# Cross-attention and mixture-of-experts layer: the key-value summary by single heads on four column tiles of TensorE, the read-out by pairs of heads on two row tiles

## The chip, the cores and the metric

The kernel runs on one core of a Trainium2 chip. The metric is device time in microseconds (us), the median of several runs; it is compared with the same kernel before the change.

## What is computed

A layer with two parts, in fp32 throughout. `x` is (4, 512, 512), `ctx` is (4, 1024, 512), there are 16 heads of 32 columns each and 8 experts.

```python
def feature(x): return where(x > 0, x + 1.0, exp(x))
# part 1: linear attention over the context
q, gate = layernorm(x) @ Wq.T, sigmoid(layernorm(x) @ Wg.T + bg)
k, v = split(ctx @ Wkv.T)                      # 16 heads x 32 columns
q, k = feature(q), feature(k)
kv_summary = einsum('bhsd,bhse->bhde', k, v)   # 32 x 32 for each head
k_sum = k.sum(axis=-2)                         # 32 for each head
z = 1.0 / (einsum('bhld,bhd->bhl', q, k_sum)[..., None] + EPS)
attn = einsum('bhld,bhde->bhle', q, kv_summary) * z
x = x + (attn * gate) @ Wo.T
# part 2: two of eight experts for each token
w, sel = top_k(layernorm(x) @ Wr, 2); w = softmax(w)
x = x + sum over the two of w * (layernorm(x) @ We[sel] + be[sel])
```

## The kernel before

The program is written engine by engine, with counting semaphores between the engines. TensorE's order of work is written out by hand in two lists, `KEYS` and `QUERIES`, which every engine walks in the same order. There are four batches. `keys(0)` comes first; then a loop of three rounds does `queries(b)` and `keys(b + 1)`; then `queries(3)`, and after it the expert part, 46 tiles of 128 rows.

`KEYS` goes over the eight context tiles of 128 rows of one batch. For each tile i it has "T c" (four transposes of the next context tile), "P k" and "P v" (the two projections), and "KV" of the tile before. In between stand the transposes "T z", the router's logits "L" (L1105) and the prefix counts "K" (L1111, L1112) of the batch before. A projection is done by `three`: each operand is split into a high and a low fp32r half, and for each of four row blocks there are three matmuls of 512 columns (L1097, L1098, L1099), 12 in all.

"KV" (L1151) adds one context tile to the key-value summary, and does so in plain fp32: four matmuls, one for each group g of four heads. The stationary operand is `khat[:, g*128:(g+1)*128]` (128 rows of context by 128 columns of keys), the moving operand is `vones[:, g, :]`, 132 columns: the four heads' 128 columns of values and four columns of ones, which give the sums of the keys. The result in PSUM (`kvp`, two groups in each of the two banks `kvb`) holds each head's keys against all four heads' values, of which only the four blocks on the diagonal are wanted. After the eighth tile VectorE multiplies it with a 0/1 `mask` into `kvbd` (L882, two operations of 264 columns). GpSimd builds `mask` at the start of the program (L468 to L475).

`QUERIES` has the four query projections "Q", then for four token tiles the gate projection "G", the read-out "A", the transposes "T a" of the attention's output, and the output projection "O". "A" (L1179) does four fp32 matmuls, one for each g: stationary `qhat[:, g, tile]` (128 features by 128 tokens), moving `kvbd[:, g, :]` (132 columns); groups 0 and 1 go to one PSUM bank, 2 and 3 to a second. VectorE then works in `attend` (L885): `den` from the last four columns of each group (L890, two operations), the reciprocal (L894), four operations that scale 128 columns each (L899), and the product with the gate (L904).

An fp32 matmul of the program is two matmul instructions and two weight loads in the profile: the 128 matmuls of "KV" are 256 instructions, the 64 of "A" are 128.

GpSimd, beside the attention, splits the expert weights and stores them to DRAM (`cut_to_dram`, L522), and computes the scales of both layer norms (L498); its first `load_expert` waits for the last of the attention's weights to be split (`w_low`, L539). SyncE (SP) issues the loads. For the expert part it issues, in one queue, the halves of the experts' weights (L373), the zero rows for padding (L365), the row tiles of each expert tile (L360) and the biases (L393).

Of the kernel before, what the change touches and what calls it, by code (L numbers as in the profile page):

```python
# [10 lines left out]
ALU = mybir.AluOpType  # L11
# [3 lines left out]
P = 128  # L15
HEADS = 16
ATTN_EPS = 1e-6
# [3 lines left out]
def xattn_moe_kernel(nc, x, ctx_in, wq_t, wg_t, bg, wkv_t, wo_t, wr, we, be, out):  # L21
# [16 lines left out]
    HG = HEADS // G  # L38
    HD = D // HEADS
    CW = P + HG  # L40
    assert L == D == 512 and ST == 8 and TT == KT == 4 and E == 8


# [13 lines left out]
    with ExitStack() as stack:  # L57
        def sb(name, shape, dt=F32):
            return stack.enter_context(nc.sbuf_tensor(name, shape, dt))
# [32 lines left out]
        BUF = 4 * D + G * 2 * CW + 2 * D  # L92
        buf = sb("buf", [P, BUF])
        ctx_raw = buf[:, 0:4 * D].rearrange("p (s t d) -> p s t d", s=2, t=2)
        vones = buf[:, 4 * D:4 * D + 2 * G * CW].rearrange("p (s g c) -> p s g c", s=2, g=G)
        expk = buf[:, 4 * D + 2 * G * CW:BUF].rearrange("p (s d) -> p s d", s=2)
        expq = expk
        be_all = buf[:, 0:E * D].rearrange("p (e d) -> p e d", e=E)
        khat = sb("khat", [P, 2, D])
        xs_raw = khat  # L100
        kvbd = sb("kvbd", [P, G, CW])
        zeros = sb("zeros", [P, D])
        bias = sb("bias", [P, D])
        y_sb = [kvbd[:, :, :].rearrange("p g c -> p (g c)")[:, 0:D], zeros[:, :]]
# [62 lines left out]
        pj = [stack.enter_context(nc.psum_tensor(f"pj{i}", [P, D], F32)) for i in range(4)]  # L167
        kvb = [stack.enter_context(nc.psum_tensor(f"kvb{i}", [P, D], F32)) for i in range(2)]
        late_z = [a[:, :].rearrange("p (k c) -> p k c", k=KT) for a in kvb]
        kvp = [a[:, 0:2 * CW].rearrange("p (g c) -> p g c", g=2) for a in kvb]  # L170


        w_loaded = [sem(f"w_loaded{i}") for i in range(2 * 4 + 3)]
# [100 lines left out]
        def pj_bank(name, i, second=0):  # L274
            return pj[place(PJ_USES, name, i, second) % 4]
# [158 lines left out]
        def _(pool):  # L434
# [20 lines left out]
            link(nc.gpsimd.affine_select(out=ident[:, :], in_=ident[:, :], compare_op=ALU.not_equal, fill=1.0,  # L455
                                         base=0, pattern=[[-1, P]], channel_multiplier=1))
            link(nc.gpsimd.memset(full[1], 1.0))
            nc.gpsimd.memset(vones[:, :, :, P:CW], 1.0).then_inc(consts, 1)
            nc.gpsimd.memset(mhalf[:, :], -0.5).then_inc(consts, 1)
            nc.gpsimd.memset(nt[:, 0:1], 0.0).then_inc(consts, 1)  # L460
            nc.gpsimd.memset(run[:, :, :], 0.0).then_inc(consts, 1)
# [9 lines left out]
            for ap, pat in ((m4, [[-HD, HG], [0, HD]]), (mask[:, P:CW], [[-HD, HG]])):  # L471
                link(nc.gpsimd.affine_select(out=ap, in_=ap, compare_op=ALU.is_ge, fill=0.0, base=0,
                                             pattern=pat, channel_multiplier=1))
                link(nc.gpsimd.affine_select(out=ap, in_=ap, compare_op=ALU.is_ge, fill=0.0, base=HD - 1,
                                             pattern=[[-s, c] for s, c in pat], channel_multiplier=-1))  # L475
            link(nc.gpsimd.memset(full[0], 0.0))

            link(nc.gpsimd.affine_select(out=full[0], in_=full[0], compare_op=ALU.is_ge, fill=1.0,
# [138 lines left out]
        def _(act):  # L617
# [43 lines left out]
            def keys(b, before_):  # L661
                for step, kind, i in KEYS:
                    if before_ is None and (step, i) in CHUNKS and kind in ("", "z"):
                        high_w(CHUNKS[step, i])
                    elif step == "T":
                        high(kind, b if kind != "z" else before_, i)
                    elif step == "P" and kind == "k":
                        act.wait_ge(SEMS["k"], nth("k", b, i))
                        act.wait_ge(SEMS["kv"], nth("kv", b, i - 2))
                        nc.scalar.activation(khat[:, i % 2, :], pj_bank("expk", i)[:, :], ACT.Relu)  # L670

                        act.wait_ge(SEMS["khat"], nth("khat", b, i - 2)) if i >= 2 else act.wait_ge(SEMS["qhat"], nth("qhat", b, i - 2))
                        nc.scalar.activation(expk[:, i % 2, :], pj_bank("expk", i)[:, :], ACT.Exp).then_inc(SEMS["expk"], 1)  # L673
                    elif step == "P":
                        act.wait_ge(SEMS["v"], nth("v", b, i))
                        act.wait_ge(SEMS["kv"], nth("kv", b, i - 2))
                        nc.scalar.copy(vones[:, i % 2, :, 0:P], pj_bank("v_copied", i)[:, :].rearrange("p (g c) -> p g c", g=G)).then_inc(SEMS["v_copied"], 1)
                        if i == 0 and before_ is not None:
                            norm_x2(before_, TT - 1)
                        if i in (4, 5):  # L680
                            norm_x(b, i - 4, before_)
                        if i == 6:
                            norm_x(b, 2, before_)
                            norm_x(b, 3, before_)
                    elif step == "L":
                        exp_gap(before_, i)
# [87 lines left out]
        def _(dve):  # L774
# [85 lines left out]
            def keys(b, before_):  # L860
                for step, kind, i in KEYS:
                    if before_ is None and (step, i) in CHUNKS and kind in ("", "z"):
                        low_w(CHUNKS[step, i])
                    elif step == "T" and kind != "z":
                        low(kind, b, i)
                    elif step == "P" and kind == "k":
                        dve.wait_ge(SEMS["expk"], nth("expk", b, i))

                        nc.vector.scalar_tensor_tensor(khat[:, i % 2, :], expk[:, i % 2, :], 1.0, khat[:, i % 2, :],  # L869
                                                       ALU.min, ALU.add).then_inc(SEMS["khat"], 1)  # L870
                    elif step == "P":
                        if i in (2, 3):
                            stats_x(b, 2 * i - 4)
                            stats_x(b, 2 * i - 3)
                    elif step == "L":
                        pick_two(before_, i, pj_bank("logit_copied", i))
                    elif step == "K":
                        rank_two(0, before_, i, pj_bank("ranked", i))
                dve.wait_ge(SEMS["kv"], nth("kv", b, ST - 1))
                for h in range(2):  # L880
                    m = mask[:, :].rearrange("p (a c) -> p a c", a=1).broadcast_to((P, 2, CW))
                    last = nc.vector.tensor_tensor(kvbd[:, 2 * h:2 * h + 2, :], kvp[h], m, ALU.mult)  # L882
                last.then_inc(SEMS["kvbd"], 1)

            def attend(b, t):  # L885

                banks = [pj_bank("ag", t, h) for h in range(2)]
                dve.wait_ge(SEMS["at"], nth("at", b, t))
                for h in range(2):
                    last = nc.vector.tensor_scalar(  # L890
                        den[:, t % 2, 8 * h:8 * h + 8].rearrange("p (g c) -> p g c", g=2),
                        banks[h][:, 0:2 * CW].rearrange("p (g c) -> p g c", g=2)[:, :, P:CW], ATTN_EPS, None, ALU.add)
                link(last)
                link(nc.vector.reciprocal(z[:, t % 2, :], den[:, t % 2, :]))  # L894
                dve.wait_ge(SEMS["t_a"], nth("t_a", b, t - 2)) if t >= 2 else dve.wait_ge(SEMS["t_x"], nth("t_x", b, TT - 1))
                for h in range(2):
                    for g in range(2):
                        zz = z[:, t % 2, 8 * h + 4 * g:8 * h + 4 * g + 4].rearrange("p (c a) -> p c a", a=1)
                        last = nc.vector.tensor_tensor(  # L899
                            num[:, t % 2, (2 * h + g) * P:(2 * h + g + 1) * P].rearrange("p (c e) -> p c e", c=HG),  # L900
                            banks[h][:, g * CW:g * CW + P].rearrange("p (c e) -> p c e", c=HG), zz.broadcast_to((P, HG, HD)), ALU.mult)
                link(last)
                dve.wait_ge(SEMS["gate"], nth("gate", b, t))
                nc.vector.tensor_tensor(num[:, t % 2, :], num[:, t % 2, :], gate[:, t, :], ALU.mult).then_inc(SEMS["ag"], 1)  # L904
# [162 lines left out]
        def _(pe):  # L1067
# [51 lines left out]
            def keys(b, before_):  # L1119
                for step, kind, i in KEYS:  # L1120
# [22 lines left out]
                    elif step == "KV":  # L1143
# [3 lines left out]
                        pe.wait_ge(SEMS["v_copied"], nth("v_copied", b, i))  # L1147
                        if i == 0:
                            pe.wait_ge(SEMS["kvbd"], nth("kvbd", b, -1))
                        for g in range(G):  # L1150
                            last = nc.tensor.matmul(kvp[g // 2][:, g % 2, :], khat[:, i % 2, g * P:(g + 1) * P], vones[:, i % 2, g, :],  # L1151
                                                    start=(i == 0 and g % 2 == 0), stop=(i == ST - 1), skip_group_check=True)
                        last.then_inc(SEMS["kv"], 1)

            def turn_m(m, slot, n):
# [6 lines left out]
            def queries(b):  # L1162
                for step, kind, i in QUERIES:
# [8 lines left out]
                    elif step == "A":  # L1172
                        if i == 0:
                            pe.wait_ge(SEMS["kvbd"], nth("kvbd", b, 0))
                            pe.wait_ge(SEMS["qhat"], nth("qhat", b, G - 1))
                        for h in range(2):
                            bank = free(PJ_USES, pj, b, "ag", i, h)
                            for g in range(2 * h, 2 * h + 2):
                                last = nc.tensor.matmul(bank[:, (g % 2) * CW:(g % 2 + 1) * CW], qhat[:, g, i * P:(i + 1) * P], kvbd[:, g, :],  # L1179
                                                        start=True, stop=True, skip_group_check=True)  # L1180
                        last.then_inc(SEMS["at"], 1)
                    elif step == "T" and kind == "c":
                        if b is LAST:
# [96 lines left out]
```

## Time and profile before

| | |
|---|---|
| median of 3 runs | 614.5 us (614.04 to 616.86) |
| the profiled execution, its own time | 615.09 us |
| its span, first to last instruction | 613.5 us |
| mean granted TensorE clock | 0.975 of 2.4 GHz |
| TensorE matmul busy | 560.7 us, 91% |
| TensorE weight load busy | 469.5 us, 77% |
| VectorE / ScalarE / GpSimd busy | 323.3 / 198.6 / 166.4 us |
| attention part / expert part | about 0 to 415 us / 415 to 613 us |

A matmul instruction's duration in the trace overlaps with the next one's: what it costs in a stream is the distance between two starts, and busy TensorE is not TensorE at its peak. "PE" rows are matmuls, "PEld" rows are the weight loads.

### The profile page before, as it was taken

Reading aid. Unit: us, or ns where it says so; the run is one execution under the profiler, and the core shown is the slowest. Engines: PE = TensorE matmul, PEld = TensorE weight load, DVE = VectorE, ACT = ScalarE, POOL = GpSimd, SP = SyncE. Lnnn points to the kernel's source line nnn. Section 1 sums busy time; section 2 is a strip of 40 time slices with the busy share of each in tenths; the row PEclk is TensorE's granted clock in tenths of the full one; section 3 lists DMA queues with packets and bytes.
Section 4 is the critical chain, followed back from the end, with each engine's and each line's share of the span. In section 5 each row is a group of like instructions: output and inputs, shape, how many; then the busy total and the mean of one; then the engine's idle time right before and its main releaser. Section 6 shows DMA issues by size and latency. Waiting matters only on the chain.

```text
span 613.5 us, 10482 instructions
## 1 busy us (share of the span) xinstructions
PE 560.7 (91%) x2944; PEld 469.5 (77%) x2945; DVE 323.3 (53%) x889; ACT 198.6 (32%) x348; POOL 166.4 (27%) x193
## 2 busy tenths in 40 slices
PE   6999997999999999999999999995999999998750
PEld 4888886788887878887887888884878788776540
DVE  4553275356337736533763642773466544457653
ACT  5455332433533353444243344422211111111100
POOL 3014654303632131356030152001022000056313
PEclk9999999999999999999999999998799999999995
DMA  8713345602452061253234125869967558789956
GB/s 281 285 35 109 132 147 197 240 35 105 168 175 103 9 230 68 103 203 105 103 94 163 51 103 204 303 197 403 413 196 238 171 169 277 240 242 363 386 191 188
DMA packets 44427, 113.87 MB, mean 186 GB/s; under 512 B 4976, under 2 KB 4976, under 8 KB 43504
## 3 DMA queue, kind: packets, MB, share of 16 engines
q1 hardware_dynamic: 24240, 57.43, 27.7%
q0 software_dynamic: 11232, 39.85, 18.2%
q10 hardware_dynamic: 8928, 16.26, 6.9%
q8 instruction: 13, 0.21, 0.1%
q14 instruction: 14, 0.11, 0.1%
HBM read 66.86 MB, written 46.66 MB: 185 GB/s over the span
## 4 chain that ended last, share of the span: by engine, by line
PE 65%; DMA 11%; issue 4%; POOL 3%; DVE 2%; ACT 1%; POOLq 0%; SPq 0%; DVEq 0%; ACTq 0%
PE pj L1097 17%; PE pj L1099 17%; PE pj L1098 17%; DMA khat<-xs 5%; PE kvb L1151 4%; PE tp L1089 4%; PE tp L1159 3%; PE pj L1105 2%; PE pj L1179 2%; POOL aux L531 1%; DMA out_dram<-wraw 1%; DMA wraw<-in_L_ffn_We_dram 1%; DMA we_halves<-aux 1%; DMA qhat<-y,gidx 1%; DMA num<-y,gidx 1%
## 5 line engine op out<-in xcount | busy, mean ns | idle before, releaser
L1097 PE MATMUL pj<-R 128*128 128x512 f32 x448 | 184.7, 412 | 9.8 <-DVE R L804 9.8
L1099 PE MATMUL pj<-R 128*128 128x512 f32 x448 | 177.0, 395 | 0.0
L1098 PE MATMUL pj<-R 128*128 128x512 f32 x448 | 175.9, 393 | 0.0
L1097 PEld LDWEIGHTS pj<-R 128*128 128x128 f32 x448 | 85.0, 190 | 26.7 <-DVE R L804 11.6
L1099 PEld LDWEIGHTS pj<-R 128*128 128x128 f32 x448 | 84.7, 189 | 19.1
L1098 PEld LDWEIGHTS pj<-R 128*128 128x128 f32 x448 | 85.3, 190 | 15.4
L1097 PE MATMUL pj<-R,aux 128*128 x184 | 77.1, 419 | 5.1 <-DVE zeros L1013 2.5
L1099 PE MATMUL pj<-R,aux 128*128 x184 | 73.0, 397 | 0.0
L1098 PE MATMUL pj<-R,aux 128*128 x184 | 72.6, 395 | 0.0
L714 ACT CAST aux<-tp 128x512 fp32r<-128x512 f32 x46 | 26.9, 586 | 118.7 <-PE tp L1159 118.7
L869 DVE SCALAR_TENSOR_TENSOR khat<-buf,khat 128x512 f32<-128x512 f32 x32 | 25.7, 803 | 69.7 <-ACT buf L673 69.7
L804 DVE TENSOR_TENSOR R<-tp,R 128x512 fp32r<-128x512 f32 x64 | 43.8, 685 | 27.4 <-ACT R L636 27.4
L498 POOL TENSOR_TENSOR rstd<-rstd,mhalf 128x1 f32<-128x1 f32 (+1 forms) x20 | 13.4, 669 | 129.2 <-DVE rstd L822 129.1
L491 POOL DMA_INDIRECT xs<-normed,xidx x16 | 15.9, 994 | 109.5 <-DVE xidx L857 107.0
L1097 PEld LDWEIGHTS pj<-R,aux 128*128 128x128 f32 x184 | 35.1, 191 | 13.2 <-issue 7.5
L596 POOL DMA_INDIRECT qhat<-y,gidx x16 | 15.9, 995 | 94.7 <-issue 75.9
L1099 PEld LDWEIGHTS pj<-R,aux 128*128 128x128 f32 x184 | 35.1, 191 | 7.7
L670 ACT ACTIVATE khat<-pj 128x512 f32<-128x512 f32 x32 | 19.2, 599 | 66.3 <-PE pj L1099 66.3
L808 DVE TENSOR_TENSOR aux<-tp,aux 128x512 fp32r<-128x512 f32 x46 | 31.8, 690 | 16.7 <-ACT aux L714 15.7
L636 ACT CAST R<-tp 128x512 fp32r<-128x512 f32 x64 | 37.6, 588 | 6.7 <-PE tp L1089 6.3
L1098 PEld LDWEIGHTS pj<-R,aux 128*128 128x128 f32 x184 | 35.3, 192 | 5.9
L1159 PE MATMUL tp<-ident,khat 128*128 128x128 f32 x184 | 28.4, 277 | 10.7 <-DMA khat<-xs 10.7
(160 smaller groups left out, 740.4 us busy)
## 6 DMA issues: line engine op xcount, KB each, us to landing
we_halves<-aux POOLq DMA_DIRECT2D x14, 1024.0 KB, 5.1
R<-we_halves SPq DMA_DIRECT2D x7, 2048.0 KB, 11.1
khat<-xs SPq DMA_DIRECT2D x46, 256.0 KB, 3.2
wraw<-in_L_ffn_We_dram POOLq DMA_DIRECT2D x16, 512.0 KB, 6.5
buf<-in_ctx_dram SPq DMA_DIRECT2D x15, 512.0 KB, 3.5
y<-kvbd ACTq DMA_DIRECT2D x23, 256.0 KB, 3.6
y<-zeros ACTq DMA_DIRECT2D x23, 256.0 KB, 3.4
wraw<-in_x_dram SPq DMA_DIRECT2D x4, 1024.0 KB, 7.7
```

The costliest lines, as they stand in the source:

```text
L636: nc.scalar.copy(dst, src).then_inc(SEMS["h_" + kind], 1)
L670: nc.scalar.activation(khat[:, i % 2, :], pj_bank("expk", i)[:, :], ACT.Relu)
L714: nc.scalar.copy(xsT_hi[:, slot, :, :], tp[slot][:, :, :]).then_inc(MOE["h_m"], 1)
L804: nc.vector.tensor_tensor(lo, tp_bank("l_" + kind, i)[:, :, :], hi.bitcast(F32), ALU.subtract).then_inc(SEMS["l_" + kind], 1)
L808: nc.vector.tensor_tensor(xsT_lo[:, slot, :, :], tp[slot][:, :, :], xsT_hi[:, slot, :, :].bitcast(F32), ALU.subtract).then_inc(MOE["l_m"], 1)
L869: nc.vector.scalar_tensor_tensor(khat[:, i % 2, :], expk[:, i % 2, :], 1.0, khat[:, i % 2, :], ALU.min, ALU.add).then_inc(SEMS["khat"], 1)
L1089: last = nc.tensor.transpose(bank[:, k, :], src[:, k * P:(k + 1) * P], ident[:, :])
L1097: nc.tensor.matmul(bank[:, :], s_hi(k), m_hi(k), start=(k == 0), stop=False)
L1098: nc.tensor.matmul(bank[:, :], s_hi(k), m_lo(k), start=False, stop=False)
L1099: last = nc.tensor.matmul(bank[:, :], s_lo(k), m_hi(k), start=False, stop=(k == KT - 1))
L1151: last = nc.tensor.matmul(kvp[g // 2][:, g % 2, :], khat[:, i % 2, g * P:(g + 1) * P], vones[:, i % 2, g, :], start=(i == 0 and g % 2 == 0 ...
L1159: last = nc.tensor.transpose(tp[slot][:, k, :], xs_raw[:, slot, k * P:(k + 1) * P], ident[:, :])
```

## The change

"KV" now works head by head. The array is used as four column tiles of 128 rows by 32 columns. For each of the 16 heads there is one fp32 matmul with the head's 32 key columns as the stationary operand and 33 moving columns (its 32 value columns and one of ones), in column tile n % 4; the result of the four heads of a group lies on four strips of 32 partitions, and all groups fit in one bank (4 x 33 columns). `vones` becomes 16 groups of 33 columns instead of 4 of 132.

`kvd` takes the place of `kvbd`: for each g and each pair of heads, 66 columns. On partitions 0 to 63 lie heads 0 and 1 of the group, on 64 to 127 heads 2 and 3; the mask is folded to match (two additions on GpSimd at the start). "A" works on two row tiles of 64 rows by 128 columns: for each g two fp32 matmuls of 66 moving columns, of 64 features by 128 tokens each, the two row tiles to different banks. VectorE reads in pairs of heads: `kvbd` is still made by two operations (of 256 and of 8 columns), `den` by two, and the scaling by two operations of 256 columns in place of four of 128. Semaphores, the order of the steps, DMAs and everything in the expert part stay.

```diff
+    PW, PC, HC = P // 2, P // 2 + HG // 2, HD + 1
...
-        vones = buf[:, 4 * D:4 * D + 2 * G * CW].rearrange("p (s g c) -> p s g c", s=2, g=G)
+        vones = buf[:, 4 * D:4 * D + 2 * G * CW].rearrange("p (s g c) -> p s g c", s=2, g=HEADS)
...
+        kvd = kvbd[:, :, :].rearrange("p g c -> p (g c)")[:, 0:G * PC].rearrange("p (g c) -> p g c", g=G)
...
-        kvp = [a[:, 0:2 * CW].rearrange("p (g c) -> p g c", g=2) for a in kvb]
+        kvp = kvb[0][:, 0:G * HC].rearrange("p (g c) -> p g c", g=G)
...
-            nc.gpsimd.memset(vones[:, :, :, P:CW], 1.0).then_inc(consts, 1)
+            nc.gpsimd.memset(vones[:, :, :, HD:HC], 1.0).then_inc(consts, 1)
...
+            link(nc.gpsimd.tensor_tensor(mask[:, 0:PW], mask[:, 0:PW], mask[:, PW:P], ALU.add))
+            link(nc.gpsimd.tensor_tensor(mask[:, PW:PC], mask[:, P:P + HG // 2], mask[:, P + HG // 2:CW], ALU.add))
...
-                        nc.scalar.copy(vones[:, i % 2, :, 0:P], pj_bank("v_copied", i)[:, :].rearrange("p (g c) -> p g c", g=G)).then_inc(SEMS["v_copied"], 1)
+                        nc.scalar.copy(vones[:, i % 2, :, 0:HD], pj_bank("v_copied", i)[:, :].rearrange("p (g c) -> p g c", g=HEADS)).then_inc(SEMS["v_copied"], 1)
...
-                for h in range(2):
-                    m = mask[:, :].rearrange("p (a c) -> p a c", a=1).broadcast_to((P, 2, CW))
-                    last = nc.vector.tensor_tensor(kvbd[:, 2 * h:2 * h + 2, :], kvp[h], m, ALU.mult)
+                for a, n, c0 in ((0, HD, 0), (HD, 1, PW)):
+                    own = mask[:, c0:c0 + HG // 2 * n].rearrange("p (a c e) -> p a c e", a=1, e=n).broadcast_to((P, G, HG // 2, n))
+                    both_heads = kvp[:, :, a:a + n].rearrange("p g (c e) -> p g c e", c=1).broadcast_to((P, G, HG // 2, n))
+                    last = nc.vector.tensor_tensor(kvd[:, :, c0:c0 + HG // 2 * n].rearrange("p g (c e) -> p g c e", e=n), both_heads, own, ALU.mult)
...
-                for h in range(2):
-                    for g in range(2):
-                        zz = z[:, t % 2, 8 * h + 4 * g:8 * h + 4 * g + 4].rearrange("p (c a) -> p c a", a=1)
-                        last = nc.vector.tensor_tensor(
-                            num[:, t % 2, (2 * h + g) * P:(2 * h + g + 1) * P].rearrange("p (c e) -> p c e", c=HG),
-                            banks[h][:, g * CW:g * CW + P].rearrange("p (c e) -> p c e", c=HG), zz.broadcast_to((P, HG, HD)), ALU.mult)
+                for r in range(2):
+                    zz = z[:, t % 2, :].rearrange("p (g r c a) -> p g r c a", g=G, r=2, a=1)[:, :, r, :, :]
+                    last = nc.vector.tensor_tensor(
+                        num[:, t % 2, :].rearrange("p (g r c e) -> p g r c e", g=G, r=2, e=HD)[:, :, r, :, :],
+                        banks[r][:, :, 0:PW].rearrange("p g (c e) -> p g c e", e=HD), zz.broadcast_to((P, G, HG // 2, HD)), ALU.mult)
...
-                        for g in range(G):
-                            last = nc.tensor.matmul(kvp[g // 2][:, g % 2, :], khat[:, i % 2, g * P:(g + 1) * P], vones[:, i % 2, g, :],
-                                                    start=(i == 0 and g % 2 == 0), stop=(i == ST - 1), skip_group_check=True)
+                        for n in range(HEADS):
+                            g, r = n // HG, n % HG
+                            last = nc.tensor.matmul(kvp[r * HD:(r + 1) * HD, g, :], khat[:, i % 2, n * HD:(n + 1) * HD], vones[:, i % 2, n, :],
+                                                    start=(i == 0 and g == 0), stop=(i == ST - 1), skip_group_check=True, tile_position=(0, r * HD))
...
-                        for h in range(2):
-                            bank = free(PJ_USES, pj, b, "ag", i, h)
-                            for g in range(2 * h, 2 * h + 2):
-                                last = nc.tensor.matmul(bank[:, (g % 2) * CW:(g % 2 + 1) * CW], qhat[:, g, i * P:(i + 1) * P], kvbd[:, g, :],
-                                                        start=True, stop=True, skip_group_check=True)
+                        banks = [free(PJ_USES, pj, b, "ag", i, r) for r in range(2)]
+                        for g in range(G):
+                            for r in range(2):
+                                last = nc.tensor.matmul(banks[r][:, g * PC:(g + 1) * PC], qhat[r * PW:(r + 1) * PW, g, i * P:(i + 1) * P],
+                                                        kvd[r * PW:(r + 1) * PW, g, :], start=True, stop=True, skip_group_check=True,
+                                                        tile_position=(r * PW, 0))
```

## Rows read from the trace of the kernel before

**Rows 1.** The page: its first line of busy times, and the slices.

```profile
PE 560.7 (91%) x2944; PEld 469.5 (77%) x2945; DVE 323.3 (53%) x889; ACT 198.6 (32%) x348; POOL 166.4 (27%) x193
...
PE   6999997999999999999999999995999999998750
```

**Rows 2.** Windows: us, busy us of each engine (instructions), granted clock, DMA share.

```profile
98.00:117.00 19.00, 14.28 (x61) 11.20 (x60) 8.70 (x19) 8.01 (x12) 9.67 (x14) 0.91 0.55 181
117.00:175.00 58.00, 57.96 (x335) 49.85 (x336) 26.66 (x105) 21.94 (x42) 17.06 (x18) 1.00 0.36 132
```

**Rows 3.** The chain that ended last: start, us, what, merged.

```profile
123.27 0.79 PE pj L1105 x8
...
170.94 1.80 PE kvb L1151 x16
...
191.10 0.90 PE pj L1179 x8
```

**Rows 4.** Groups by form: count, busy us, mean ns.

```profile
L1151 PE MATMUL kvb<-buf,khat 128*128 128x132 f32 x256 | 34.7, 281 | 0.0
...
L1179 PE MATMUL pj<-kvbd,qhat 128*128 128x132 f32 x128 | 17.2, 277 | 1.4 <-DVE qhat L926 1.4
```

**Rows 5.** Timeline around one "L" and "KV", TensorE: start, us, engine, line.

```profile
122.66 0.39 PE L1098 MATMUL pj<-R 128*128 128x512 f32 x1
122.88 0.39 PE L1099 MATMUL pj<-R 128*128 128x512 f32 x1
123.11 0.95 PE L1105 MATMUL pj<-wr_sb,qhat 128*128 128x8 f32 x8
...
125.26 0.47 PE L1097 MATMUL pj<-R 128*128 128x512 f32 x1
125.57 0.40 PE L1098 MATMUL pj<-R 128*128 128x512 f32 x1
```

**Rows 6.** Timeline around one "K", the router's prefix counts.

```profile
132.09 0.17 PE L1111 MATMUL pj<-members,before 128*128 128x8 bf16 x1
132.09 0.10 PEld L1112 LDWEIGHTS pj<-members,ones 128*128 128x128 bf16 x1
132.12 0.17 PE L1112 MATMUL pj<-members,ones 128*128 128x8 bf16 x1
```

**Rows 7.** Windows of L1151 alone, batch 0's keys: matmul busy (count), loads.

```profile
0.00:50.00 50.00, 5.33 (x40) 5.27 (x40) 1.00 0.54 185
50.00:66.00 16.00, 3.03 (x24) 2.93 (x24) 1.00 0.39 133
```

**Rows 8.** One line's instructions: L795, the split of the attention's weights.

```profile
L795 DVE TENSOR_TENSOR R<-wraw,R x12: 682/693/694, 5.0 to 50.3; 128x512 fp32r<-128x512 f32 x12
...
  POOL wraw L504: 13.2, 1
```

**Rows 9.** Timeline of TensorE's two long idle stretches (idle before, releaser).

```profile
104.60 0.50 PE L1097 MATMUL pj<-R 128*128 128x512 f32 x1 [3.33 <-DVE R L804]
...
106.84 0.63 PE L1097 MATMUL pj<-R 128*128 128x512 f32 x1
107.26 0.63 PE L1098 MATMUL pj<-R 128*128 128x512 f32 x1
...
429.97 1.12 PE L1159 MATMUL tp<-ident,khat 128*128 128x128 f32 x4 [8.08 <-DMA khat<-xs]
```

**Rows 10.** Timeline of the attend step on VectorE, and the transposes after it.

```profile
188.38 0.24 DVE L890 TENSOR_SCALAR den<-pj 128x8 f32<-128x8 f32 x2 [0.83 <-PE pj L1179]
...
188.94 0.88 DVE L899 TENSOR_TENSOR num<-pj,z 128x128 f32<-128x128 f32 x4
189.85 0.69 DVE L904 TENSOR_TENSOR num<-num,gate 128x512 f32<-128x512 f32 x1
...
191.84 0.60 PE L1089 MATMUL tp<-ident,num 128*128 128x128 f32 x4
```

**Rows 11.** Timeline: the mask on VectorE, GpSimd's last constant, the first load of "KV".

```profile
7.27 0.29 POOL L484 CAST ones<-num 128x128 bf16<-128x128 f32 x1
...
20.63 1.10 PEld L1151 LDWEIGHTS kvb<-buf,khat 128*128 128x128 f32 x8
...
172.78 0.77 DVE L882 TENSOR_TENSOR kvbd<-kvb,mask 128x264 f32<-128x264 f32 x2 [0.44 <-PE kvb L1151]
```

More of the change, by code:

```diff
@@ L879, in keys @@
                 dve.wait_ge(SEMS["kv"], nth("kv", b, ST - 1))
-                for h in range(2):
-                    m = mask[:, :].rearrange("p (a c) -> p a c", a=1).broadcast_to((P, 2, CW))
-                    last = nc.vector.tensor_tensor(kvbd[:, 2 * h:2 * h + 2, :], kvp[h], m, ALU.mult)
+                for a, n, c0 in ((0, HD, 0), (HD, 1, PW)):
+                    own = mask[:, c0:c0 + HG // 2 * n].rearrange("p (a c e) -> p a c e", a=1, e=n).broadcast_to((P, G, HG // 2, n))
+                    both_heads = kvp[:, :, a:a + n].rearrange("p g (c e) -> p g c e", c=1).broadcast_to((P, G, HG // 2, n))
+                    last = nc.vector.tensor_tensor(kvd[:, :, c0:c0 + HG // 2 * n].rearrange("p g (c e) -> p g c e", e=n), both_heads, own, ALU.mult)
                 last.then_inc(SEMS["kvbd"], 1)
             def attend(b, t):
-                banks = [pj_bank("ag", t, h) for h in range(2)]
+                banks = [pj_bank("ag", t, r)[:, 0:G * PC].rearrange("p (g c) -> p g c", g=G) for r in range(2)]
                 dve.wait_ge(SEMS["at"], nth("at", b, t))
-                for h in range(2):
+                for r in range(2):
                     last = nc.vector.tensor_scalar(
-                        den[:, t % 2, 8 * h:8 * h + 8].rearrange("p (g c) -> p g c", g=2),
-                        banks[h][:, 0:2 * CW].rearrange("p (g c) -> p g c", g=2)[:, :, P:CW], ATTN_EPS, None, ALU.add)
+                        den[:, t % 2, :].rearrange("p (g r c) -> p g r c", g=G, r=2)[:, :, r, :],
+                        banks[r][:, :, PW:PC], ATTN_EPS, None, ALU.add)
                 link(last)
@@ L1175, in queries @@
                             pe.wait_ge(SEMS["qhat"], nth("qhat", b, G - 1))
-                        for h in range(2):
-                            bank = free(PJ_USES, pj, b, "ag", i, h)
-                            for g in range(2 * h, 2 * h + 2):
-                                last = nc.tensor.matmul(bank[:, (g % 2) * CW:(g % 2 + 1) * CW], qhat[:, g, i * P:(i + 1) * P], kvbd[:, g, :],
-                                                        start=True, stop=True, skip_group_check=True)
+                        banks = [free(PJ_USES, pj, b, "ag", i, r) for r in range(2)]
+                        for g in range(G):
+                            for r in range(2):
+                                last = nc.tensor.matmul(banks[r][:, g * PC:(g + 1) * PC], qhat[r * PW:(r + 1) * PW, g, i * P:(i + 1) * P],
+                                                        kvd[r * PW:(r + 1) * PW, g, :], start=True, stop=True, skip_group_check=True,
+                                                        tile_position=(r * PW, 0))
                         last.then_inc(SEMS["at"], 1)
```

## The prediction

> **What bounds the kernel now.** I read the page first: TensorE's matmuls are busy for 560.7 of 613.5 us, and only a few of the 40 slices fall below 9 tenths [rows 1]. The windows then say how full: from 117 to 175 us, 57.96 of 58.00 us are busy at a granted clock of 1.00 [rows 2]. So in the attention part a nanosecond of TensorE is a nanosecond of the end, apart from two idle stretches, to which I come below. The chain of waits agrees: "KV" and "A" both stand on it [rows 3]. The other engines wait for TensorE, so what the change saves them is worth nothing by itself.
>
> **What "KV" and "A" cost now.** Start to start, eight instructions of "A" take 0.90 us and sixteen of "KV" 1.80 us [rows 3]: 112.5 ns for a pair of weight load and matmul, so 0.90 us for a visit of "KV" (8 pairs) and the same for one of "A". Their own durations of 281 and 277 ns [rows 4] overlap and are not the price. Which half of a pair sets the 112.5 ns? "L" answers it: the same fp32 load of 128 columns, but only 8 moving columns, and its eight pairs are 0.79 us for seven distances, 113 ns [rows 3]. So 124 moving columns fewer change nothing: the load sets the rhythm already, and the stream of 132 columns takes at most as long. This is what the reader should keep in mind. Shorter streams, or streams side by side, gain nothing unless the loads get cheaper too.
>
> **"KV" after.** A visit becomes 16 fp32 matmuls, so 32 pairs, with 32 stationary and 33 moving columns. The columns loaded are the same as before (16 x 32 = 4 x 128), and so are the columns streamed (16 x 33 = 4 x 132). If both go by columns, a load is 113 x 32/128 = 28 ns and a stream 112.5 x 33/132 = 28 ns. The quickest pair in the trace is that of "K": the next matmul starts 30 ns after, with its load between [rows 6]. I take 30 ns: 32 x 0.030 = 0.96 us, +0.06 us for a visit. Bound above: a load of 32 columns costs as much as one of 128, 32 x 0.113 = 3.6 us, +2.7 us. Bound below: the four tiles of a group work side by side, loads too, 8 x 0.028 = 0.22 us, -0.68 us.
>
> **"A" after.** A visit becomes 8 fp32 matmuls, 16 pairs, each with 128 stationary columns on 64 rows, and 66 moving ones. The stream halves, but the number of columns to load doubles. With loads one after another it is 16 x 0.111 = 1.78 us (the load's share of a pair, a little under 113), +0.88 us for a visit. Bound below: the two row tiles load side by side, 0.9 us, no change. No row shows loads in parallel, so I take the upper one.
>
> **Changing the shape of the array.** Each visit goes from the full array to tiles and back. The trace has no tiles. It has changes between kinds of matmul: the first fp32r matmul after fp32 ones starts 0.31 us before the next instead of 0.22 [rows 5], so 0.09 us. I take 0.1 us a change, 0.2 us a visit. Bound below: nothing. Bound above: the array has to run empty, which is the part of a matmul that overlaps with the next (0.39 - 0.22 = 0.17 us [rows 5]), and the next load, 0.11 us, stands alone: 0.28 us a change, 0.56 a visit.
>
> The Trainium skill, "TensorEngine Tiling (Array Packing)", section Tiling Modes, says that changing the tiling mode drains TensorE. By that rule the upper bound would hold; no row here shows it.
>
> **Which visits count.** There are 32 of "KV" and 16 of "A". Batch 0's last three "KV" visits (24 of its 64 instructions come after 50 us [rows 7]) and its four "A" lie before TensorE's idle 3.33 us at 101 to 104.6 us. That idle is not TensorE's doing: it waits for GpSimd, whose chain of expert weights starts with the last split of the attention's weights at 50.3 us [rows 8]. After it eight matmuls run 0.43 us apart instead of 0.23 [rows 9], 1.6 us more, at half clock (1.2 GHz). So 3.33 + 1.6 = 4.9 us of cover, against 3 x 0.26 + 4 x 1.08 = 5.1 us: about all of it vanishes there. The last batch's four "A" lie before 8.08 us of waiting for a row tile [rows 9], behind 4 MB of expert weights in the same queue; 4.3 us vanish there too. Without these covers 9 us would be added. What is left: 29 visits of "KV" and 8 of "A".
>
> **The other edits, at nothing.** `attend` has two scaling operations for four that take 0.88 us; the mask's two of 264 columns take 0.77 us [rows 11], so 0.1 us less. The step ends at 190.54 us and the transposes that read it start at 191.84 [rows 10]: it was hidden and stays so. The mask's step gets some 0.2 us shorter, and "A" needs it 12 us later. ScalarE's copy of the values moves the same 512 columns. GpSimd's two more operations come before 7.6 us, and the first "KV" is at 20.6 [rows 11]; at about 0.3 us each there are 13 us of cover. "A" asks for both banks before its first matmul; the second was free already. No DMA and no semaphore changes, so nothing is queued anew. TensorE gets 32 x 24 + 16 x 8 = 896 more matmuls and as many loads.
>
> **The sum.** 29 x 0.06 = 1.7; 8 x 0.88 = 7.0; 37 x 0.2 = 7.4: together +16 us on the profiled execution's 615.1, so 631. The median of the runs shown is 0.6 lower: 630.6.
>
> **The rivals.**
>
> *A. Faster: tiles load and stream side by side.* What speaks for it is that the four heads of a group touch different columns of the array. Against it: loads run one by one in every row here, and the two passes of one head still follow each other. With the two passes in sequence and only different heads overlapping, a "KV" is 16 x 0.028 = 0.45 us, -0.45 x 29 = -13; "A" at 0.9 adds nothing; changes free: 602. With changes at 0.2 us, 609; with all eight rounds in parallel, 595. It decides once a "KV" visit falls below 0.90 - (7.4 + 7.0)/29 = 0.40 us, or below 0.65 if "A" stays at 0.9.
>
> "TensorE: Matmul & The Clock Gate" of the Trainium skill, section Part 3, Measured speedup vs the span model, has 2.38 times for three column tiles, at 512 columns. With as much for 33 columns, "KV" would be about 0.4 us, an estimate from that page.
>
> *B. The array empties at each change.* The matmuls' visible tail of 0.17 us speaks for it, the cheap change at 125.3 us against it. 37 x 0.56 = 20.7 in place of 7.4: 644.
>
> *C. Small loads have a floor.* If a pair cannot go below some 56 ns, half of a full one, "KV" is 1.8 us, +0.9 x 29 = +26, with "A" and the changes 655; at the full 113 ns, +77, over 700. Against it: the 30 ns pair of "K", though that is bf16.
>
> *D. Nothing measurable.* Same columns loaded, row tiles loaded side by side, changes free: 614 to 617. The change then does its overlap only where loads hide it.
>
> **How the numbers follow.** Forecast 0.34, A 0.24, B 0.18, C 0.11, D 0.13. A time within 0.5% (3 us) of 614.5 is about what a measurement cannot tell from no change. Slower by more: forecast, B and C, 0.63. Within: D, 0.13. Faster: A, 0.24. Range: from A's middle, 602, to above B, 650; out are C and the better half of A, about 2 in 10. The forecast's own range is 622 to 638.
>
> **What would show it.** In the profile after, L1151 should have 1024 matmuls and L1179 256. The distance between their starts is the test: 30 ns in "KV" (0.96 us a visit) and 111 ns in "A" (1.78 us). Right after each visit the first fp32r matmul should stand 0.3 us before the second; a gap before the first load of a visit speaks for B. The idle before 104.6 us should be nearly gone, and that at 430 us be about 4 us. Starts of different heads a few ns apart would prove A. I am wrong above all if loads of different tiles overlap, for then the premise that the load sets the rhythm fails, or if a change of shape costs several times 0.1 us.

## The result: 1.1% faster, where I had forecast 2.6% slower

The changed kernel takes 609.37 us (median of 4 runs, 607.55 to 610.86) against 615.68 us before: a ratio of 0.9891, 95% interval 0.9858 to 0.9924. The fourth series, below, gave 0.992 (0.9891 to 0.9948). My forecast of 630.6 us was wrong in sign. The case that came true is the rival A, a gain, and of its three prices the one in which changes of shape are not free (609). That the time meets this price so closely is luck: a visit of "KV" became cheaper than rival A had it, and some 5 us were then lost in waits and in the clock that rival A did not have.

The page of the changed kernel, its lines beside [rows 1]:

```profile
PE 552.5 (91%) x3840; PEld 450.7 (74%) x3841; DVE 324.3 (53%) x857; ACT 197.8 (32%) x348; POOL 167.3 (27%) x195
...
PE   5999997999999999999999999995899999998750
```

TensorE has 896 matmuls more, as foreseen, and 8 us less busy time, which was not. The groups by form (count, busy us, mean ns), beside [rows 4]:

```profile
L1184 PE MATMUL pj<-kvbd,qhat 64*128 64x66 f32 x256 | 17.8, 278 | 2.5 <-DVE qhat L930 2.5
L1156 PE MATMUL kvb<-buf,khat 128*32 128x33 f32 x1024 | 14.5, 198 | 0.0
```

The 1024 matmuls of "KV" are busy 14.5 us in all; the 256 before were 34.7. That is 14 ns each, where I had put 30. The chain of waits, start and length in us, beside [rows 3]:

```profile
121.30 0.39 PE kvb L1156 x32
121.69 0.59 PE tp L1093 x4
...
129.08 0.39 PE kvb L1156 x32
...
187.92 1.04 PE pj L1184 x16
```

A visit of "KV" is 0.39 us of matmuls (it was 0.90 to 1.0), a visit of "A" 1.04 us (it was 0.90). The timeline shows the edges of a visit:

```profile
157.58 0.39 PE L1102 MATMUL pj<-R 128*128 128x512 f32 x1
157.80 0.39 PE L1103 MATMUL pj<-R 128*128 128x512 f32 x1
158.12 0.35 PEld L1156 LDWEIGHTS kvb<-buf,khat 128*32 128x32 f32 x32 [0.35 <-issue]
158.12 0.46 PE L1156 MATMUL kvb<-buf,khat 128*32 128x33 f32 x32
...
158.51 0.42 PEld L1093 LDWEIGHTS tp<-ident,normed 128*128 128x128 f32 x4
158.51 0.66 PE L1093 MATMUL tp<-ident,normed 128*128 128x128 f32 x4
```

The last projection matmul starts at 157.80, so the next could start at 158.03; the first of "KV" starts at 158.12. It comes 0.09 us late, and its load is not pulled ahead under the matmul before it: the loads' row stands idle 0.35 us. In the kernel before, the first load of such a visit starts at 27.49 us and its matmul at 27.72, so the load lay 0.23 us ahead. A change of the array's shape does cost something. Behind the visit it costs more: in the chain the four transposes after it take 0.59 us, where the transposes with no visit ahead of them take 0.44.

The best single measure is the distance between the same points of two rounds, which needs no account of edges. Three rounds of `KEYS` in batch 1 take 24.70 us before (first matmul of "KV" at 123.92 and 148.62) and 23.32 after (121.23 and 144.55): 0.46 us less a visit. In batch 0, where the next projection and not a transpose follows on "KV", it is 0.31 us less (6.86 us a round, then 6.55). Two rounds with "A" take 10.92 us before (190.94 to 201.86) and 11.46 after (187.85 to 199.31): 0.27 us more a visit. What the shape itself costs is what is left over: 0.51 us of matmuls are saved in a "KV" (0.90 to 0.39; behind "L", where the old visit took 1.00, it is 0.61), and 0.46 us arrive behind "L" and 0.31 in batch 0, so 0.15 to 0.20 us a visit; "A" has 0.14 us more of matmuls and 0.27 in all, so 0.13. All positions below are read in this way from the timelines.

### The profile page after: what moved, and what is told of

Read it like the earlier page. It is cut to its first block, busy times and chain, and to the rows that moved or that the text cites. A ratio compares the mean times of both kernels' runs of the same rounds, so it can differ in the third digit from the quotient of the medians.

```text
span 608.9 us, 12257 instructions
## 1 busy us (share of the span) xinstructions
PE 552.5 (91%) x3840; PEld 450.7 (74%) x3841; DVE 324.3 (53%) x857; ACT 197.8 (32%) x348; POOL 167.3 (27%) x195
## 4 chain that ended last, share of the span: by engine, by line
PE 62%; DMA 12%; issue 5%; DVE 4%; POOL 3%; ACT 2%; POOLq 0%; DVEq 0%; ACTq 0%; SPq 0%
PE pj L1101 17%; PE pj L1103 16%; PE pj L1102 16%; PE tp L1093 4%; DMA khat<-xs 4%; DMA y<-zeros 3%; PE tp L1164 2%; PE pj L1184 2%; PE pj L1109 2%; POOL aux L535 1%; DMA wraw<-in_L_ffn_We_dram 1%; PE kvb L1156 1%; DMA qhat<-y,gidx 1%; DMA we_halves<-aux 1%; DVE qhat L930 1%
## 5 line engine op out<-in xcount | busy, mean ns | idle before, releaser
L873 DVE SCALAR_TENSOR_TENSOR khat<-buf,khat 128x512 f32<-128x512 f32 x32 | 27.3, 854 | 58.1 <-ACT buf L677 58.0
L495 POOL DMA_INDIRECT xs<-normed,xidx x16 | 18.1, 1130 | 106.9 <-DVE xidx L861 104.4
```

The costliest lines, as they stand in the source:

```text
L495: nc.gpsimd.indirect_dma_start(out=xs_dram[g][:, :], out_offset=bass.IndirectOffsetOnAxis(ap=xidx[:, t, j:j + 1], axis=0), in_=xn[t], in_o ...
```

## Experiments

The rival theories are told with each run. With the result there are four series. In the third the kernel before took 621.3 us, in the others 615.7 to 616.5, so across series only ratios are compared.

**One part alone.** `e1_kv_only` keeps the summary on column tiles and puts the read-out back:

```diff
-                for a, n, c0 in ((0, HD, 0), (HD, 1, PW)):
+                for a, n, c0 in ((0, HD, 0), (HD, 1, P)):
...
-                        banks = [free(PJ_USES, pj, b, "ag", i, r) for r in range(2)]
...
+                        for h in range(2):
+                            bank = free(PJ_USES, pj, b, "ag", i, h)
+                            for g in range(2 * h, 2 * h + 2):
+                                last = nc.tensor.matmul(bank[:, (g % 2) * CW:(g % 2 + 1) * CW], qhat[:, g, i * P:(i + 1) * P], kvbd[:, g, :],
+                                                        start=True, stop=True, skip_group_check=True)
```

> The key-value summary on four column tiles as in the change; the mask's step, attend and the read-out as before (full array, 132 columns). Theory 1 (the gain comes from the summary alone, and the read-out on row tiles gives part of it back): a summary visit stays at 0.39 us of matmuls as in the changed kernel, a read-out visit goes back to 0.90 us from 1.04 plus 0.1; 8 to 12 visits that count make 2 to 4 us less than the changed kernel, 605 to 607 us. Theory 2 (the two parts gain together, or the gain lies elsewhere, in the shorter VectorE steps): no less than the changed kernel's 609 us.

0.9898 (0.9848 to 0.9948). Two rounds with "A" are back at 10.92 us. The whole gain is in the summary. The time, 609.3 us, is not the 605 to 607 of the first theory. Whether the read-out gives part of it back this series could not resolve; the last one did.

`e2_a_only` does the reverse: the summary as before, the read-out on row tiles.

> The read-out on two row tiles as in the change, the summary as before (four matmuls of 132 columns). Theory 1: 16 pairs in 1.04 us and a gap of 0.1 us before them, 0.2 to 0.3 us more a visit; with 8 visits that count 2 to 3 us slower than before, 616 to 618 us. Theory 2: as fast as before or faster. My forecast's term for this part alone was +7.0 and 8 x 0.2 us, which would be 623 us.

1.0025 (0.9992 to 1.0058), and 0.27 us more for each visit of "A" in the trace (188.76 to 200.22 us for two rounds). By itself this part does not help, and it is far from the 623 us of my forecast's terms; that it costs at all is shown by the trace only.

**The order of the tiles.** This is the run that decides about my premise. `e3_kv_same_tile` issues the same 16 matmuls, but four heads on one column tile, then four on the next:

```diff
-                            g, r = n // HG, n % HG
+                            r, g = n // G, n % G
```

> The changed kernel with the summary's 16 heads in another order: the four heads of one column tile one after the other, then the next tile. Same matmuls, same sums. Theory 1 (neighbouring instructions overlap because they go to different column tiles): three of four heads now follow one on the same tile, pairs 25 to 30 ns apart, a visit of 0.7 to 0.9 us instead of 0.39, 9 to 15 us more than the changed kernel, 618 to 624 us. Theory 2 (a pair of 32 and 33 columns is as cheap as 12 ns by itself, whichever tile): 0.39 us as before, 609 us.

1.002 (0.998 to 1.0061): the gain is gone. The chain, start and length:

```profile
161.92 0.83 PE kvb L1156 x31
```

0.83 us instead of 0.39 for the same matmuls, 27 ns a pair. So the columns do set a pair's price as I had thought (28 ns), as long as neighbours share a tile. Where they alternate, loads and streams of different tiles overlap, and a pair costs 12 ns. `e4_a_same_tile` turns the read-out's loops in the same way:

```diff
-                        for g in range(G):
-                            for r in range(2):
+                        for r in range(2):
+                            for g in range(G):
```

> The changed kernel with the read-out's order turned: the four groups on row tile 0, then the four on row tile 1. Same for the read-out: if the overlap comes from alternating row tiles, 16 loads of 128 columns follow one another at 111 ns, 1.6 to 1.8 us instead of 1.04, 5 to 8 us more than the changed kernel (8 to 12 visits), 614 to 617 us. If loads on 64 rows are cheap by themselves: 1.04 us and 609 us.

0.9987 (0.9949 to 1.0024), about 1% above the changed kernel's ratio. The chain:

```profile
189.09 1.54 PE pj L1184 x16
...
193.95 1.54 PE pj L1184 x16
```

96 ns a pair on the same row tile, 65 ns (1.04 / 16) when they alternate. My 111 ns lies 15% above the first number, and the kernel does not pay even that one.

`e9_pairs` works the summary by pairs of heads on two column tiles of 64 columns, half as many instructions:

```diff
-                        for n in range(HEADS):
-                            g, r = n // HG, n % HG
+                        for n in range(2 * G):
+                            g, r = n // 2, n % 2
```

> The changed kernel with the summary by pairs of heads on two column tiles of 64 columns (8 fp32 matmuls of 64 stationary and 66 moving columns, 16 pairs of load and matmul) in place of 16 on four tiles. Theory 1 (a pair costs its columns over the number of neighbouring tiles that overlap): 56 ns a pair alone, 28 ns overlapped by two, but the two passes of one head in sequence as well, between 0.45 and 0.65 us a visit against 0.39: 2 to 7 us more than the changed kernel. Theory 2 (the 12 ns of a pair are the rate at which instructions are issued, and half as many instructions take half as long): 0.2 us a visit, 5 us less, 604 us.

0.9985 (0.9956 to 1.0014), in the third series. The timeline:

```profile
161.18 0.69 PE L1154 MATMUL kvb<-buf,khat 128*64 128x66 f32 x16
161.80 0.66 PE L1091 MATMUL tp<-ident,normed 128*128 128x128 f32 x4
```

A visit is 0.61 to 0.62 us (161.18 to 161.80), 38 ns a pair. Half the instructions take longer, not shorter, so a visit's time does not go by the number of instructions. Whether the 12 ns of the smaller pairs are themselves a limit of issue, this run does not separate, since its pairs are twice as large. Two tiles overlap less than four: 56 ns (an estimate by columns, half of 112.5) become 38, a factor of 1.5, where 27 become 12, a factor of 2.2. The row tiles have 96 to 65, 1.5 again. In all of them the two passes of one fp32 matmul follow each other on the same tile; that this is what keeps the factor below the number of tiles is an inference, and no run here separates it.

**The price of a change of shape.** `e5_split` cuts 28 visits of "KV" in two:

```diff
+                        elif i >= 1:
+                            half_kv(b, i - 1, range(0, HEADS // 2), before_)
...
+                        if i == ST - 1:
+                            half_kv(b, i, range(0, HEADS // 2), before_)
+                        half_kv(b, i, range(HEADS // 2, HEADS), None).then_inc(SEMS["kv"], 1)
```

> The changed kernel with each summary visit but the eighth of a batch cut in two: heads 0 to 7 before the value projection of the next context tile, heads 8 to 15 at the old place. Same matmuls; 28 more visits, so 28 more changes to column tiles and back (a batch's eighth visit stays whole). Theory 1 (a change of the array's shape has a price of its own): each half should show 0.2 us of matmuls and, again, a gap of about 0.09 us before its first load and 0.05 to 0.15 us more behind it: 0.15 to 0.25 us for each added visit, 25 of them on the path, 4 to 6 us longer, span 613 to 615 us. Theory 2 (the gap belongs to the semaphore wait and not to the shape): only the visit with the wait has it, and the time stays near 609 us. My rival B's price of 0.56 us a visit would be 14 us.

One execution, 625.89 us, with the kernel before at 621.3 beside it. The timeline:

```profile
143.62 0.60 PE L1093 MATMUL tp<-ident,buf 128*128 128x128 f32 x4
144.15 0.33 PE L1133 MATMUL kvb<-buf,khat 128*32 128x33 f32 x16
144.41 0.50 PE L1101 MATMUL pj<-R 128*128 128x512 f32 x1
144.75 0.40 PE L1102 MATMUL pj<-R 128*128 128x512 f32 x1
...
162.09 0.39 PE L1103 MATMUL pj<-R 128*128 128x512 f32 x1
162.40 0.33 PE L1133 MATMUL kvb<-buf,khat 128*32 128x33 f32 x16
```

The gap is there again (the transposes' 0.44 us end at 144.06), though nothing is waited for at this point. The visit at 162.40 settles it: second halves have no wait for a semaphore in the program at all, and it starts 0.31 us after the last projection matmul instead of 0.23. So the gap belongs to the shape. Half the matmuls take 0.26 us, not 0.2. From the second half of batch 1's first visit to that of its seventh it is 46.19 us (123.94 to 170.13) where the changed kernel needs 44.26 (121.23 to 165.49): 0.32 us for each of six added visits. Rival B's 0.56 is ruled out, and "free" as well. Of the 0.32, 0.13 are the matmuls, which take 2 x 0.26 us in two halves and 0.39 in one piece; 0.19 are the edges. My 0.2 for a visit that was there before is therefore about right, and an added visit costs 0.32.

**Where part of the gain went.** In the changed kernel TensorE waits after each batch's last "KV", and did not before:

```profile
167.09 0.49 PE L1101 MATMUL pj<-R 128*128 128x512 f32 x1 [0.74 <-DVE R L808]
...
371.33 0.86 PE L1156 MATMUL kvb<-buf,khat 128*32 128x33 f32 x64
372.85 0.50 PE L1101 MATMUL pj<-R 128*128 128x512 f32 x1 [0.66 <-DVE R L808]
```

The query projections need the split of the last transposes of x, which stand just ahead of two visits of "KV". Those used to cover it with 1.8 us and now do with 0.8. `e6_tx3` moves the transposes:

```diff
-        KEYS += [("P", "k", i), ("T", "c", i + 1) if i + 1 < ST else ("T", "x", 2), ("P", "v", i)]
+        KEYS += [("P", "k", i), ("T", "c", i + 1) if i + 1 < ST else ("T", "x", 2)]
+        KEYS += [("T", "x", 3)] if i == ST - 1 else []
+        KEYS += [("P", "v", i)]
...
-        KEYS += [("T", "x", 3)] if i == ST - 1 else []
```

> The changed kernel with the last transposes of x (T x 3) ahead of the last value projection instead of behind it. In the changed kernel TensorE waits 0.74 us in each batch after the eighth summary visit for the split of these transposes, which two summary visits of 0.9 us used to cover. Theory 1 (part of the gain was turned into this wait): the wait goes, 3 to 4 times 0.74 us, 606 to 607 us. Theory 2 (the wait only moves to the next stage, the query projections' ScalarE and VectorE work): unchanged, 609 us.

0.988 (0.9822 to 0.9939), no difference that this resolves. The timeline shows why:

```profile
166.62 0.46 PE L1157 MATMUL kvb<-buf,khat 128*32 128x33 f32 x32
167.46 0.46 PE L1157 MATMUL kvb<-buf,khat 128*32 128x33 f32 x32 [0.38 <-ACT buf L682]
168.20 0.49 PE L1102 MATMUL pj<-R 128*128 128x512 f32 x1 [0.28 <-issue]
```

The 0.74 us became 0.38 for ScalarE's copy of the values, which the last "KV" needs at once, and 0.28 more, for which the trace names no engine. The wait for VectorE before the first "A" grew as well, from 1.29 to 1.60 us in batch 1 and from 1.25 to 1.39 in batch 2. The period from the second "A" of batch 2 to that of batch 3 is 100.49 us against the changed kernel's 100.72.

**The version that beats both.** `e7_kv_only_tx3` has the read-out of `e1_kv_only` and the order of `e6_tx3`.

> The summary on column tiles, the read-out on the full array, and T x 3 ahead of the last value projection. If both earlier effects add up (read-out 2 to 3 us cheaper, 2 to 3 us of waits gone) it is the fastest so far, 604 to 606 us. If the time given back is in neither, 609 us as the changed kernel.

0.9866 (0.9807 to 0.9925), 612.69 us beside 621.3, the lowest of its series. Because these intervals overlap, the three candidates were run once more in one series.

> The changed kernel once more, as the measure for the next two on the same chip. 0.985 to 0.992 of the kernel before, if the first measurement was right.

> The summary on column tiles, the read-out on the full array, as in the first series. By the traces each read-out visit is 0.27 us shorter than in the changed kernel; if 8 to 12 of them count, 0.35 to 0.5% less than the changed kernel. If the stretch before the expert part, where TensorE waits for the experts' weights, or batch 0's wait for GpSimd takes it back, the two are the same within 0.2%.

> As the run before, with T x 3 ahead of the last value projection. In the traces this gave back only 0.25 of the 0.74 us of each batch, because the wait for VectorE was followed by one of 0.38 us for ScalarE's copy of the values; 4 x 0.25 = 1 us, 0.15% less than the run before, which this measurement may not resolve. Against the changed kernel: 0.4 to 0.7% less if both count in full.

| fourth series | median us | ratio to before | 95% interval |
|---|---|---|---|
| the change (`r1_after`) | 612.82 | 0.992 | 0.9891 to 0.9948 |
| summary alone on tiles (`r1_kv_only`) | 608.55 | 0.9857 | 0.9832 to 0.9882 |
| the same, T x 3 earlier (`r1_kv_only_tx3`) | 607.28 | 0.9834 | 0.9812 to 0.9856 |

The change without its second half is 0.6% faster than the whole change, in intervals that do not overlap. The last row lies 0.2% below the one before it; their intervals overlap.

## Why the prediction was wrong

**How far ahead of the kernel before, along the run.** From the timelines of the profiled executions, at the start of each point, in us:

| point | before, at | the change | `r1_kv_only_tx3` |
|---|---|---|---|
| fourth "A" of batch 0 | 93.36 | 1.1 | 1.3 |
| first "KV" of batch 1 | 123.92 | 2.7 | 0.7 |
| last two "KV" of batch 1 | 170.78 | 5.3 | 3.3 |
| second "A" of batch 1 | 190.94 | 3.1 | 3.4 |
| last two "KV" of batch 2 | 274.09 | 4.9 | 5.9 |
| fourth "A" of batch 2 | 304.93 | 3.5 | 5.5 |
| last two "KV" of batch 3 | 377.16 | 5.8 | 8.1 |
| fourth "A" of batch 3 | 407.16 | 5.0 | 8.5 |
| end of the span | 613.5 | 4.6 | 6.0 |

**"KV" after: the step that failed.** It said that loads go one after another and took 30 ns a pair, 0.96 us a visit and +0.06. Measured: 12 ns, 0.39 us, so -0.51 instead of +0.06. From "L" I had read rightly that a full load sets the rhythm of the full array; all rows of the trace have all loads on the same tile, and I carried this over to four. `e3_kv_same_tile` shows that the rule by columns holds on one tile (27 ns) and fails across tiles. I had priced the overlap at 0.45 us as rival A, and its chance of 0.24 was too low for something that no row could exclude. The old visit was also too cheap in my account where it follows on "L": the chain before has 1.00 us there, not 0.90. The Trainium skill, "TensorE: Matmul & The Clock Gate", Part 3, Measured speedup vs the span model, has the 2.38 times from which I had estimated 0.4 us a visit. The trace agrees: 0.39 us, 2.1 times less than the 0.83 of the same matmuls tile by tile.

**"A" after: right in sign, its term sized wrong.** +0.88 us for 16 loads in a row, measured +0.14 (1.04 for 0.90): the row tiles overlap too, and even tile by tile (`e4_a_same_tile`) a pair takes 96 ns and not my 111; with the edges a visit costs 0.27 us more instead of 1.08. For 8 visits this is 2.2 us and not 8.6.

**Changing shape: right.** 0.2 us a visit, measured 0.15 to 0.20 for "KV" and 0.13 for "A" against the kernel before, and 0.32 for a visit that is added. The Trainium skill's rule in "TensorEngine Tiling (Array Packing)", Tiling Modes, that a change of mode drains TensorE, fits the load that is not pulled ahead; the price is well below the 0.56 us that I had worked out for a full emptying.

**The sum with measured terms.** In batches 1 to 3 a "KV" visit saves 0.43 us on average (44.26 for 46.86 us over six rounds), in batch 0 0.31. With 0.41 for the 29 visits of my count it is -12; 8 x 0.27 is +2: some -10 us, where the profiled pair shows 4.6 and the medians 6.3. About half was given back, at four places. First, the new wait after each batch's last "KV", 0.74 us three times and 0.66 once. Second, a longer wait for VectorE before the first "A" of batches 1 and 2, 1.29 and 1.25 us where it was 0.78 and 0.57. Third, half a clock: after the first "A" of batch 1 nine matmuls run 0.43 us apart, 1.6 us in all. The windows (us, busy us of each engine, granted clock, DMA):

```profile
175.00:183.40 8.40, 7.11 (x44) 5.69 (x42) 3.81 (x3) 4.08 (x6) 4.66 (x4) 1.00 0.41 141
183.40:187.10 3.70, 3.70 (x10) 2.92 (x11) 1.94 (x6) 0.00 (x0) 0.17 (x1) 0.54 0.97 314
```

The clock falls to its lower level (1.2 GHz) after an idle 1.29 us and 16 matmuls on row tiles, and the distance from first to second "A" is 5.59 us, where batch 2 has 3.98. No simple rule comes out of the traces. Batch 2 of the same profile, and of `e6_tx3`, have the same sequence and keep the full clock (the last line is of `e6_tx3`):

```profile
182.26 1.11 PE L1184 MATMUL pj<-kvbd,qhat 64*128 64x66 f32 x16 [1.29 <-DVE qhat L930]
...
285.98 1.11 PE L1184 MATMUL pj<-kvbd,qhat 64*128 64x66 f32 x16 [1.25 <-DVE qhat L930]
...
287.48 1.11 PE L1185 MATMUL pj<-kvbd,qhat 64*128 64x66 f32 x16 [1.39 <-DVE qhat L931]
```

Over all profiles, row tiles after an idle of 1.16 us or more are followed by the fall five times (1.29, 1.64, 1.60, and in `e4_a_same_tile` 1.64 and 1.21 us) and not three times (1.16, 1.25 and 1.39 us). It never follows after 1.02 us or less, nor with the read-out on the full array in five places after 1.06 to 1.39 us. So neither the length of the idle nor the tiles sort the cases by themselves, and what decides stays open.

Fourth, the expert part: it begins with a wait for the experts' weights, 6.57 us after and 8.11 in `r1_kv_only_tx3`, and of 8.5 us of lead at the end of the attention that kernel keeps 6.0; the change keeps 4.6 of 5.0. Against these stand 1.6 us of clock that the changed kernel's profile won at batch 0's idle, told next.

**The covers.** I had said that batch 0's last three "KV" and its four "A" count for nothing. The idle did not go, for there was nothing to fill it: it is 3.04 us in the changed kernel's profile. There the lead even grew across it, from 1.1 to 2.7 us: GpSimd's last scale before the idle ends came 1.2 us earlier than in the kernel before, and the eight slow matmuls behind it (1.6 us) were absent. Their absence is chance. In `r1_after`, the same kernel in another execution, they are there again (104.07 to 106.99 us), and the lead at the first "KV" of batch 1 is 0.8. In `r1_kv_only_tx3` it fell from 1.3 to 0.7, with 3.89 us of idle and slow matmuls after it, and in `e1_kv_only` from 1.8 to nothing. So a lead at that point is worth what GpSimd's chain and the clock leave of it, and one trace of before was no base for a count. The last batch's "A" did lie before a long wait for DMA, as foreseen.

**The other edits.** VectorE's scaling takes 0.76 us for 0.88, on no path, as said. Nothing showed for GpSimd's two operations.

## What to carry to other kernels

Whether work on tiles of the array pays is decided by the order of issue: let neighbouring matmuls go to different tiles, and price them by measured pairs, 12 ns for 128x32 in four tiles, 27 on one. The shape adds 0.13 to 0.20 us to a visit that was there before, and a visit that is added costs 0.32; the tiles have to save more than that, which four column tiles did (0.9 to 0.39 us) and two row tiles with a full-width load did not (0.90 to 1.04). After making one step on the critical path shorter, look at what it used to cover: here the split of the last transposes, and then the copy of the values.

## What was not expected of the hardware

- Weight loads of different column tiles overlap with each other: 32 loads of 32 fp32 columns start within 0.39 us, against 0.83 us on the same tile. With two tiles of 64 columns it is 38 ns a pair, with two row tiles 65 instead of 96.
- TensorE took 32 pairs of load and matmul, 64 instructions, in 0.39 us: 6 ns an instruction.
- The granted clock fell to its lower level after an idle of as little as 1.21 us followed by matmuls on row tiles, in five of eight such places, and in none of five with the full array (1.06 to 1.39 us of idle). Two places in one profile with 1.29 and 1.25 us of idle and the same matmuls differ, and what decides is open.
